# An attention block whose buffer of exponentials goes from four key tiles to eight

## The reference, cut to what matters

```python
def _L0_attn_ref(x, ln_gamma, ln_beta, w_qkv, b_qkv, w_out, b_out):
    h = (x - mu) * rsqrt(var + 1e-05) * ln_gamma + ln_beta
    q, k, v = (h @ w_qkv + b_qkv) split into 16 heads of 64
    scores = einsum('bhqd,bhkd->bhqk', q, k) / sqrt(64)
    attn = softmax(scores, axis=-1)
    out = einsum('bhqk,bhkd->bhqd', attn, v)
    return x + out.reshape(B, T, C) @ w_out + b_out

x = layernorm(x + attn_ref(x))
x = layernorm(x + ffn_ref(x))     # 1024 -> 64 -> 64 x 16, relu -> 64 -> 1024
```

## Time and profile before

| | us |
|---|---|
| three runs of the kernel | 2081.42, 2126.66, 2241.49 |
| their median | 2126.66 |
| the profiled execution | 2084.34 |
| its span on the slowest core (core 5) | 2082.8 |
| spans of the eight cores | 2065.7 to 2082.8 |
| first to last exponential, start to start (core 5) | 228.5 to 1741.3 |
| ACT busy in L845, 1024 instructions | 1143.3 |
| PE busy | 1437.4 (69% of the span) |
| ACT busy | 1278.3 (61%) |
| DVE busy | 634.6 (30%) |
| mean granted TensorE clock, core 5 | 0.885 |

### The profile page before, as it was taken

The page is one execution under the profiler, slowest core; times in us unless marked ns, Lnnn a source line. Parts: engine busy times, 40 slices in busy tenths (PEclk is TensorE's granted clock), DMA queues, the critical chain, the costliest instruction groups (busy, mean ns, idle before and its releaser), DMA issues. The chain is left out here.

```text
span 2082.8 us, 26536 instructions; the slowest of 8 cores (2065.7 to 2082.8 us)
## 1 busy us (share of the span) xinstructions
PE 1437.4 (69%) x8552; PEld 508.1 (24%) x8552; DVE 634.6 (30%) x870; ACT 1278.3 (61%) x1254; POOL 26.1 (1%) x35
## 2 busy tenths in 40 slices
PE   1444698688858976886789588868975673465343
PEld 0221233223312322332223123223321221122111
DVE  3664222312231222123122312221231100444555
ACT  1432587677858876876778588768866884112122
POOL 0000000000000000000000000000000000000000
PEclk9875799989999999999999899999998987666555
DMA  6331000100000010001000100100000004202202
GB/s 100 120 101 31 0 6 1 11 1 6 6 6 6 1 11 1 6 1 11 1 6 1 11 1 6 11 0 6 1 1 1 1 1 78 54 1 81 73 8 81
DMA packets 44595, 44.34 MB, mean 21 GB/s; under 512 B 34993, under 2 KB 35122, under 8 KB 44466
## 3 DMA queue, kind: packets, MB, share of 16 engines
q1 hardware_dynamic: 16162, 33.72, 5.3%
q0 software_dynamic: 28304, 8.92, 4.4%
HBM read 43.16 MB, written 8.39 MB: 25 GB/s over the span
## 5 line engine op out<-in xcount | busy, mean ns | idle before, releaser
L845 ACT ACTIVATE PT_sb<-score_ps,negB_sb 128x1024 bf16<-128x1024 f32 x1024 | 1143.3, 1117 | 293.4 <-PE z_ps L787 156.2
L761 PE MATMUL score_ps<-qT_sb,kT_sb 64*128 64x512 bf16 x1024 | 398.9, 393 | 243.0 <-ACT PT_sb L845 149.8
L777 PE MATMUL pv_ps<-PT_sb,v_sb 128*64 128x512 bf16 x1024 | 405.5, 396 | 42.5 <-DVE attnT_sb L803 28.4
L781 PE MATMUL pv_ps<-PT_sb,v_sb 128*64 128x512 bf16 x1024 | 406.5, 397 | 0.0
L763 PE MATMUL score_ps<-qT_sb,kT_sb 64*128 64x512 bf16 x1024 | 403.3, 397 | 0.0
L787 PE MATMUL z_ps<-PT_sb,onesb_sb 128*64 128x512 bf16 x1024 | 394.2, 385 | 0.0
L784 PE MATMUL z_ps<-PT_sb,onesb_sb 128*64 128x512 bf16 x1024 | 394.1, 385 | 0.0
L616 PE MATMUL qkv_ps<-xhq_sb,wq_sb 128*128 128x512 bf16 x1120 | 300.1, 392 | 10.9 <-DVE kT_sb L631 5.6
L761 PEld LDWEIGHTS score_ps<-qT_sb,kT_sb 64*128 64x128 bf16 x1024 | 94.1, 93 | 626.7 <-issue 625.9
L777 PEld LDWEIGHTS pv_ps<-PT_sb,v_sb 128*64 128x64 bf16 x1024 | 111.7, 109 | 220.1 <-issue 169.5
L800 DVE RECIPROCAL zb_sb<-z_ps 128x512 f32<-128x512 f32 x32 | 107.4, 3358 | 156.2 <-PE z_ps L787 115.8
(11 more groups left out here) (81 smaller groups left out, 820.1 us busy)
## 6 DMA issues: line engine op xcount, KB each, us to landing
xtile_sb<-x SPq DMA_DIRECT2D x32, 512.0 KB, 4.2
xres_sb<-x SPq DMA_DIRECT2D x16, 512.0 KB, 8.4
out<-u_sb SPq DMA_DIRECT2D x16, 512.0 KB, 3.6
wq_sb<-wqkv POOLq DMA_DIRECT2D x24, 256.0 KB, 6.1
wout_sb<-wout POOLq DMA_DIRECT2D x1, 2048.0 KB, 22.9
win_sb<-win POOLq DMA_DIRECT2D x1, 128.0 KB, 23.0
rw_sb<-rw POOLq DMA_DIRECT2D x1, 128.0 KB, 23.0
w2b_sb<-w2b POOLq DMA_DIRECT2D x1, 128.0 KB, 23.2
```

The lines of the kernel that those rows point to most:

```text
L761: e.matmul(o, w, r, start=True, stop=True))
L777: a=s0, b=s1: e.matmul(o, w, r, start=a, stop=b, skip_group_check=True))
L781: e.matmul(o, w, r, start=a, stop=b, skip_group_check=True))
L845: e.activation(out=o, in_=i_, func=AF.Exp, bias=b, scale=0.125))
```

## The change

`PT_sb` gets eight slots instead of four: 16 KB for each partition instead of 8 KB. The slot index becomes `kt % 8` where it is written and where it is read, and the guard ahead of E(kt) waits for P(kt-8) instead of P(kt-4); for the first eight key tiles of a row it waits for the P of the row before, 24 + kt. No instruction is added, removed or moved on any engine, and S, the accumulators and the generator stay as they are. For kt = 4 to 7 of a row the second `sc.wait` is new.

```diff
-                PT_sb=SB12("PT_sb", [128, 4 * 1024], BF16),
+                PT_sb=SB12("PT_sb", [128, 8 * 1024], BF16),
...
     def emit_pvz(qt, kt, it, exp_done_ref=None):
-        spar = kt % 4
+        spar = kt % 8
...
-            spar = kt % 4
+            spar = kt % 8
             pt = PT_sb[:, spar * 1024:spar * 1024 + 1024]
             g1 = sc_done[kt]
-            if kt >= 4:
-                g1 = max(g1, pvz_done[kt - 4])
+            if kt >= 8:
+                g1 = max(g1, pvz_done[kt - 8])
             sc.wait("scalar", st, g1)
-            if kt < 4 and it >= 1:
+            if kt < 8 and it >= 1:
                 sc.wait("scalar", st,
-                        it_hist[it - 1]["pvz_done"][NKT - 4 + kt])
+                        it_hist[it - 1]["pvz_done"][NKT - 8 + kt])
```

## The result

The changed kernel takes 2039.9 us (median of 10 runs) against 2080.4 us for the kernel before (median of 10): a ratio of 0.981, with a 95% interval of 0.980 to 0.982. The forecast was 37.4 us less, a ratio of 0.982, and a time of 2047 us counted from the profiled execution at 2084.3 us. Two of each kernel's ten runs were slow ones (2126.7 and 2241.5 us before; 2169.5 and 2177.7 after, with a lower clock on one die), which the medians count and the ratio leaves out.

A forecast was written before the change was run, and what follows sets the result against it. Exponentials keep ACT busy 1143.3 of 2082.8 us, its idle time mostly waits for L787. Terms 28.0 + 8.2 + 0.7 + 0.5 = 37.4 us off 2084.3 give 2047 us; own range 2040 to 2055, wider range 2028 to 2080.

The forecast's parts named there:

- The guard can never come last: Exponentials' slot guard: the P waited for stands on the PE ahead of the S that E(kt) needs anyway.
- Place 1: Steady stretch of a query tile: exponentials keep ACT's pace, 0.31 us gained for six tiles, 28.0 us together.
- The margin: Steady stretch: the PE's lag of 0.48 plus 0.60 to E makes 1.08, below 1.21, leaving 0.13 us.
- Place 2: Change of query tile: E(4) follows E(3) directly, E(5) then waits for S(5); 0.39 us each, 8.2 for 21.
- The two small terms: Changes of query tile: 0.7 us for the first tiles of pairs 0 to 6, 0.5 us for pair 7.
- Place 3: Bound stretch, fourth query tile: PE and DVE set 3.41 us for two tiles, so no gain; bounds 0 and 56.
- New costs: Second wait instruction at kt = 4 to 7: 0, as the same pair at kt = 1 to 3 costs nothing.
- The sum: Whole kernel: 37.4 us less than the profiled 2084.3, giving 2047 us, 1.8% less; chance 0.65.
- Full release: Rival: all waits of the steady stretch and the changes of query tile go, 71 us less, 2013; chance 0.08.
- the PE taking over: Rival: in the steady stretch E waits for the scores instead, which gives nothing there; 2075 us, chance 0.20.
- The slowing by the clock: Rival: the PE's clock falls after stops at changes of query tile, 2.8 us each, 59 in all; 2106, chance 0.05.
- The faster pace: Rival: back-to-back exponentials overlap, some 1040 ns a tile instead of 1209, the PE sets the pace; near 2005, chance 0.02.

The follow-up runs named there:

- Held at the row change: Eight slots with guard P(kt-8), but E(4) of each row still waits for P(0); 0.987 of the kernel before.
- with only those freed: Eight slots, guard P(kt-4) from kt = 5 on and none at kt = 4; 0.993 of the kernel before.
- the four-slot run with the moved wait: Kernel before, with the PE's wait for DVE's reduction moved from behind a bound matmul to ahead of the next one; 0.969, 2013.7 us.
- the two halves: Two eight-slot runs with the old guard partly back: one frees only the row change (0.993 of the kernel before), one all but that (0.987).
- the extra matmul: One more overwritten 128x512 matmul ahead of each projection group; changed kernel with it 0.983, kernel before with it 1.009, both against the kernel before.

## Why the prediction was right

- **The guard can never come last.** Right: of 156.2 us of waits for L787 0.4 are left, in a place where the guard cannot be what ended them, and with five slots 0.8.
- **Place 1, 28.0 us.** Right in mechanism and nearly in size: 26.7 us in the first three tiles against 25.8, and the two steps of the one six in the fourth fell to 1.21 us as well. Held at the row change, the run gained 25.6 us from first to last exponential, with the handicaps told above. The margin that decided it was put at 0.13 us and read at 0.18; with 0.21 us more in each projection group, overruns of up to 0.1 us appeared, so the margin is real and small.
- **Place 2, 8.2 + 0.7 + 0.5 us.** Right for the 8.2: E(4) closes up, E(5) takes over the wait, and 8.8 us came of it. The two small terms were wrong. Pair 7 gave 2.0 us, not 0.5, and not at the row changes: with only those freed it gave 0.1, with them held 1.2. Its low clock stretches hold up P as well (seven waits for L787, 7.2 us, on core 5 before), which I had not gone through query tile by query tile. The first tiles of the pairs gained nothing at E(4) and E(5): E(0) to E(6), summed over the seven pairs, took 62.9 us against 62.3, where 0.7 less had been forecast. In the example of pair 4 on core 5, E(5) starts 8.04 us behind E(0) after the change,

```profile
978.11 4.73 ACT L845 ACTIVATE PT_sb<-score_ps,negB_sb 128x1024 bf16<-128x1024 f32 x4 [0.59 <-DVE negB_sb L732]
...
986.15 4.73 ACT L845 ACTIVATE PT_sb<-score_ps,negB_sb 128x1024 bf16<-128x1024 f32 x4 [1.27 <-PE score_ps L763]
```

  and before it 7.80: E(4) at 1005.07, E(5) 1.21 later, and E(0) at 998.48:

```profile
998.48 4.74 ACT L845 ACTIVATE PT_sb<-score_ps,negB_sb 128x1024 bf16<-128x1024 f32 x4 [0.58 <-DVE negB_sb L732]
```

  The granted clock goes with it: from a pair's last exponential to E(6) of the next it was 0.72 in the mean of the cores after the change and 0.74 before. That the clock is the cause is likely and not shown.
- **Place 3, nothing.** Right: 3.41 us for two tiles in both kernels, and the four-slot run with the moved wait shows whose limit it was.
- **New costs, 0.** Off by little: the second wait instruction costs nothing where ACT is the limit, as at kt = 1 to 3, but some 0.05 us where ACT then waits for the PE. That is once in each of some 30 rows of tiles, so about 1.5 us; the run with eight slots and the old guard, which has this cost and no gain, took 1.7 us more from first to last exponential than the kernel before.
- **The sum.** 39.3 us from first to last exponential against 37.4, and 40.5 between the medians. 2039.9 lies 0.1 us below the forecast's own range (2040 to 2055) and 7 us below 2047: the forecast started from an execution 4 us slower than the median of the kernel before, and the gain was 3 us larger.
- **The rivals.** Full release and the PE taking over are ruled out by the two halves and by the extra matmul. The slowing by the clock did not come: over all cores the clock fell at 6 of the 168 changes of query tile before (the prediction counted one of 21, on core 5) and at none after. It would have outweighed the 37.4 us from 14 changes on, at the prediction's 2.8 us each, not from 13. The mean clocks of the cores are 0.881 to 0.888, against 0.884 to 0.890. The faster pace by the Trainium skill's rule (ScalarE: Activation LUTs, section What ACT_TABLE_LOAD costs) did not come either: freed of all other waits, the exponentials keep 1.207 us, 1.114 and a gap of 0.09, each waiting for the one before. No run took that chained wait away, so whether they would overlap without it is not shown here.

## What to carry to other kernels

A wait that a profile names is only the last of several; ask for each place what the same instruction would wait for next. Here 156 us of a named wait were worth 40, and 61 of what was left hung on one wait of the PE for a reduction that it did not yet need. Where engines run in program order, a deeper buffer helps as far as it moves the guard behind something that must be waited for anyway (one slot was enough here); beyond that it helps only if the order of the consumer is changed as well. Before counting on a freed engine, add up the PE's work over the whole period of its pattern, and its lag within it, separately.

## What was not expected of the hardware

In each of these two profiled executions one core's exponentials took 0.2% longer from start to start in the medians (1.209 against 1.207 us on the other seven): core 5 in the kernel before, core 7 in the changed one. In the ten experiments no core did. On core 5 the exponentials were busy 2.5 us less after the change, about what this alone makes, of the 41.1 us between the two kernels from first to last exponential; so the means of all cores are to be compared beside the slowest one's. What sets it, the runs do not tell.

The extra matmul, which only adds work to the PE, went with a higher clock: the cores had 0.893 and 0.894 in the mean of the two kernels' runs, where the kernel before, run beside them, had 0.888. Why, the runs do not tell.
